# Context products moved between the stages of a four-block decoder, and paired score rows in its ReLU layer

## The chip, the cores and the metric

The program runs on one core of one Trainium2 chip. All data is float32. The metric is the device time of one execution in microseconds (us); kernels are compared by the median of several executions.

The engines are named as the profile names them: PE is TensorE's matrix multiplication and PEld its weight loads, DVE is VectorE, ACT is ScalarE, POOL is GpSimd, SP is the engine that issues the transfers here. SBUF is the on-chip memory, PSUM the matmuls' output memory, HBM the outside memory.

## The reference, cut to what matters

A decoder with four blocks works on `x` of 16 x 64 rows with 512 values. Every block has three parts: attention, attention to a second sequence (the context), and a feed-forward layer. Each part gets the layer-normalised `x` and its result is added to `x`:

```python
x = x + L0_attn(ln(x));  x = x + L0_xattn(ln(x), ctx);  x = x + L0_ffn(ln(x))
x = x + L1_attn(ln(x));  x = x + L1_xattn(ln(x), ctx);  x = x + L1_ffn(ln(x))
x = x + L2_attn(ln(x));  x = x + L2_xattn(ln(x), ctx);  x = x + L2_ffn(ln(x))
x = x + L3_attn(ln(x));  x = x + L3_xattn(ln(x), ctx);  x = x + L3_ffn(ln(x))
```

The parts that the change touches compute this:

- `L1_attn`, `L2_attn`: causal attention, 32 query heads over 8 key heads, 16 values per head. `L2_attn` also turns queries and keys by position (rotary).
- `L1_xattn`: attention to the context with 32 heads of 128 values, with a bias per head and a mask. Its keys `ctx @ Wk` and values `ctx @ Wv` depend on the context alone.
- `L2_xattn`: attention with one head of 512 values; `q = xn @ Wq.T + bq`, `k = ctx @ Wk.T + bk`, and the values are the context itself. `k` depends on the context alone too.
- `L1_ffn`: `h = relu(xn @ w1.T) * keep`, `out = h @ w2t`. `keep` is 1 for one of every 32 hidden values: the one with the largest score in `xn @ c1.T @ c2.T`, a product of rank 16.

## The kernel before

The 1024 rows of `x` stay in SBUF as eight tiles of 128 rows. The kernel is a row of stages, one after another, with a barrier between two of them, and almost every stage walks over the eight tiles. Each engine has its own program in a stage; the order on an engine is the order in which the code is written, and semaphores order the engines against each other. There is no scheduler. The stages, with the names that tiles of theirs carry in the profile: `l0a`, `l0x`, `l0f` (first block), `l1a`, `l1x`, `l1f` (second), `l2a`, `l2x`, `l2f` (third), `l3a`, `l3x`, `l3f` (fourth).

**Context products of `l1x`.** The keys and values of the biased attention are computed ahead, in earlier stages, and stored in HBM. There are 128 units: eight groups of eight key units and eight value units. Helper `Fill` (L2000 on) holds them: `unit` is the TensorE work (a key unit has 4 matmuls of 128 columns by 512, a value unit 8 of 64 columns by 512), `copy` or `copy_act` brings the result from PSUM to SBUF on VectorE or ScalarE, `store` issues the transfer to HBM and behind the last unit of a kind the load of the next group's weights. Two numbers say which stage does which unit: `l0x` does `HELD` to `HELD_X`, 72 to 112, and `l0f` does 113 to 127. In `l0x` five units stand in the opening, four at the end, and 32 in the tiles, one behind each of the four steps of a tile (`WITHIN`, called at the end of a step as `filled(n, c, 1)`):

```python
BEFORE, WITHIN = KC + 1, {(0, 1): 0, (1, 1): 1, (2, 1): 2, (3, 1): 3}
```

A step of `l0x` is: transposition of a softmaxed key block (`turn`, into the one bank `l0x_pt`, copied out by ScalarE before the next one), keys of the next tile, transposition, queries of the next tile, transposition, context product, transposition, values of the next tile.

**The two small attentions** `l1a` and `l2a` are one function, `stage_small_attn` (L3668). On TensorE a tile `n` of the loop is: projections of tile `n+1` (`project`), transposition of the normalised tile `n+2`, output projection of tile `n-1` (`out`), in `l2a` the two rotation products, the probabilities of tile `n` turned in two halves (`turns`, L3787), scores of tile `n+1` first half (`scores`, L3778), attention product of tile `n` (L3799), scores second half. VectorE does the softmax of a tile in 12 passes, in `l2a` also the rotation of the next tile; it can't start before the scores. ScalarE does the exponentials and copies; between the two exponentials of a tile stand the copies of the next tile's queries, keys and values.

**`l2x`** (`stage_l2_xattn`, L3266) loads five weights and inputs at its start and for each tile projects the queries and the keys (16 matmuls of 128 by 128 each), adds the biases on ScalarE, takes the scores, softmax, the transposed probabilities, and the product with the context. The normalisation of tile `n+1` stands ahead of the exponential of tile `n` on ScalarE. Its transposition is followed by the projections on TensorE, and both stand between the scores and the transposition of the probabilities:

```python
pe.wait_ge(q_biased, n + 2); pe.wait_ge(k_biased, n + 2)     # scores of tile n, L3331
...
f.turn(pe, n + 1); project(n + 1, 1 - u)                      # L3314, L3322
pe.wait_ge(p_ready, n + 2)                                    # then transpose p, L3338
```

**`l1f`** (`stage_l1_ffn`, L2550) works on four chunks of 448 hidden values for each tile. For each chunk TensorE does 4 matmuls of 128 by 448 (`l1f_ph`, L2609) and one score matmul with 16 rows (`l1f_pi`, L2614) from the rank-16 product `low`; VectorE finds the largest score of each 32 and masks the hidden values. Both `ph` and `pi` have two banks, used in turn.

## Time and profile before

| | us |
|---|---|
| median of three runs (lowest, highest) | 4292.85 (4287.7, 4294.64) |
| the profiled execution's own time | 4291.77 |
| its span in the trace | 4289.9 |
| PE busy in the span | 3957.4 (92%) |
| DVE busy | 2181.7 (51%) |
| ACT busy | 1427.2 (33%) |
| DMA queue q1, share of 16 engines | 14.2% |
| mean granted TensorE clock of the span | 0.96 of full speed |

The stages that the change touches lie, by the names in the trace, at about 600 to 1065 us (`l0x`), 1065 to 1215 (`l0f`), 1215 to 1380 (`l1a`), 1960 to 2230 (`l1f`), 2230 to 2428 (`l2a`) and 2428 to 2536 (`l2x`).

The profile takes one execution. A float32 matmul of the code appears as two MATMUL instructions in the trace ("x8" for 4 matmuls). Their ends are modelled and neighbouring matmuls overlap, so what a group of matmuls costs is read from its start to the start of the next group behind it, not from its duration. The granted clock is the share of full speed that TensorE was allowed: it has two levels, 1.2 and 2.4 GHz, and a mean between 0.5 and 1 says that a stretch had both.

### The profile page before, as it was taken

The numbers are of one execution on the slowest core, as the hardware profiler recorded it, in microseconds if no ns is written. First come the engines' busy times: TensorE is split into PE (matmuls) and PEld (weight loads), VectorE is DVE, ScalarE is ACT, GpSimd is POOL, SyncE is SP. The second block draws the span as 40 slices with busy tenths as digits, with TensorE's granted clock in tenths as the row PEclk, the third lists the DMA queues.
The fourth block names the chain that finished last, engine by engine and source line by source line (L and its number), as shares of the span: only waits on it lengthen the run. The fifth ranks groups of instructions, "written<-read, shape, count | busy, mean of one in ns | idle before, by whom it ended". The sixth has DMA issues, their size and how long they took to land. (4 is left out here: it accounts for less than half of the span.)

```text
span 4289.9 us, 50949 instructions
## 1 busy us (share of the span) xinstructions
PE 3957.4 (92%) x18954; PEld 2122.3 (49%) x18954; DVE 2181.7 (51%) x3810; ACT 1427.2 (33%) x2586; POOL 313.2 (7%) x288
## 2 busy tenths in 40 slices
PE   8788989998988999999988779699999999999997
PEld 3333335554455555554446564355555445555554
DVE  0887755552247322224548418865655555444433
ACT  3777735552223211111113234311111133322232
POOL 1011002111001000000000111000000000000000
PEclk9999999999988999999998889999999999999998
DMA  4111121112001423211000121111001011111100
GB/s 184 44 40 36 60 68 38 35 35 72 30 28 50 161 101 108 99 35 70 0 27 1 40 100 34 46 41 40 20 20 40 1 66 35 35 35 40 55 15 23
DMA packets 133914, 215.09 MB, mean 50 GB/s; under 512 B 42704, under 2 KB 95056, under 8 KB 123072
## 3 DMA queue, kind: packets, MB, share of 16 engines
q1 hardware_dynamic: 133696, 212.06, 14.2%
q8 instruction: 152, 2.49, 0.2%
q14 instruction: 66, 0.54, 0.0%
HBM read 167.99 MB, written 44.04 MB: 49 GB/s over the span
## 5 line engine op out<-in xcount | busy, mean ns | idle before, releaser
L930 PE MATMUL l3a_po<-l3a_wo,l3a_cT 128*128 128x512 f32 x512 | 230.7, 604 | 3.1 <-ACT l3a_cT L1067 2.9
L436 PE MATMUL l1x_pj<-kvT,l1x_wq 128*128 128x512 f32 x512 | 228.3, 599 | 0.7 <-ACT kvT L240 0.7
L481 PE MATMUL l1x_po<-l1x_wo,l1x_cT 128*128 128x512 f32 x512 | 226.2, 596 | 1.2 <-issue 1.2
L819 PE MATMUL l3x_pj<-kvT,l3x_wq 128*128 128x512 f32 x512 | 225.5, 594 | 0.0
L819 PE MATMUL l3a_pj<-kvT,l3a_wq 128*128 128x512 f32 x512 | 224.9, 592 | 0.0
L577 DVE TENSOR_TENSOR x<-x,l1x_po 128x512 f32<-128x512 f32 x64 | 44.1, 689 | 266.9 <-PE l1x_po L481 266.9
L930 PEld LDWEIGHTS l3a_po<-l3a_wo,l3a_cT 128*128 128x128 f32 x512 | 95.6, 192 | 121.4 <-issue 110.9
L819 PEld LDWEIGHTS l3a_pj<-kvT,l3a_wq 128*128 128x128 f32 x512 | 95.5, 190 | 111.5 <-issue 111.4
L819 PEld LDWEIGHTS l3x_pj<-kvT,l3x_wq 128*128 128x128 f32 x512 | 95.5, 190 | 111.4 <-issue 111.4
L481 PEld LDWEIGHTS l1x_po<-l1x_wo,l1x_cT 128*128 128x128 f32 x512 | 95.7, 192 | 110.9 <-issue 110.9
L436 PEld LDWEIGHTS l1x_pj<-kvT,l1x_wq 128*128 128x128 f32 x512 | 94.6, 190 | 110.2 <-issue 107.2
L194 POOL TENSOR_TENSOR norm_rstd<-norm_half,minus_half 128x1 f32<-128x1 f32 x70 | 42.4, 607 | 1358.9 <-DVE norm_half L189 1358.9
L930 PE MATMUL l3x_po<-l3x_wo,l3x_cT 128*128 128x512 f32 x256 | 117.6, 602 | 0.7 <-issue 0.7
L930 PE MATMUL l3x_pc<-l3x_wo,l3x_cT 128*128 128x512 f32 x256 | 115.1, 592 | 0.0
L1196 DVE TENSOR_TENSOR x<-x,l3a_po 128x512 f32<-128x512 f32 x56 | 38.5, 687 | 149.6 <-PE l3a_po L930 149.6
L1631 ACT ACTIVATE l0a_signs<-l0a_lowest_a,l0a_scalars 128x1376 uint16<-128x1376 uint16 x68 | 98.1, 1442 | 47.9 <-DVE l0a_lowest_a L1755 47.1
L531 ACT COPY l1x_cT<-l1x_pa 128x512 f32<-128x512 f32 x64 | 34.4, 589 | 238.4 <-PE l1x_pa L470 238.4
L1740 DVE TENSOR_SCALAR_CACHE_REDUCE l0a_keep<-l0a_keep,l0a_scalars 128x1376 uint16<-128x1376 uint16 x64 | 105.4, 1646 | 3.2 <-DVE l0a_scalars L1746 1.1
L2609 PE MATMUL l1f_ph<-l1f_w,l1f_xT 128*128 128x448 f32 x256 | 104.1, 550 | 1.3 <-DMA l1f_w<-in_L_ffn_w 1.3
L2637 PE MATMUL l1f_po<-l1f_w,l1f_hT 128*128 128x512 f32 x224 | 102.4, 603 | 0.0
L2045 DVE COPY l0x_fill_kv<-l0x_fill 128x512 f32<-128x512 f32 x41 | 28.4, 692 | 144.6 <-PE l0x_fill L2035 92.0
L1740 DVE TENSOR_SCALAR_CACHE_REDUCE l0a_keep<-l0a_a,l0a_scalars 128x1376 uint16<-128x1376 uint16 x60 | 98.8, 1646 | 4.1 <-DVE l0a_scalars L1746 2.1
(529 smaller groups left out, 7760.0 us busy)
## 6 DMA issues: line engine op xcount, KB each, us to landing
l1x_kb<-l1x_keys SPq DMA_DIRECT2D x32, 512.0 KB, 4.8
l1x_vb<-l1x_values SPq DMA_DIRECT2D x32, 512.0 KB, 3.4
l1x_keys<-l0a_kv SPq DMA_DIRECT2D x40, 256.0 KB, 2.0
fill_wk<-in_L_xattn_Wk SPq DMA_DIRECT2D x8, 1024.0 KB, 5.5
kvT<-in_L_xattn_Wv SPq DMA_DIRECT2D x8, 1024.0 KB, 5.8
l1x_values<-l0a_kv SPq DMA_DIRECT2D x32, 256.0 KB, 2.3
l1x_wq<-in_L_xattn_Wq SPq DMA_DIRECT2D x8, 1024.0 KB, 4.9
l1x_sbias<-in_L_xattn_bias SPq DMA_DIRECT2D x8, 1024.0 KB, 7.4
```

Of the source, the lines that this page charges most:

```text
L194: self.nc.gpsimd.tensor_tensor(self.rstd[:, t:t + 1], self.half[:, t:t + 1], self.m.minus_half[:, 0:1], ALU.pow).then_inc(self.root_ready, 1)
L436: mm = pe.matmul(pj[:, j, :], wq[:, u, k, h * DH:(h + 1) * DH], m.kvT[:, k, 1, 512 * j:512 * (j + 1)], start=k == 0, stop=k == KC - 1)
L481: mm = pe.matmul(po[:, t % 2, :], cT[:, u, h, t * P:(t + 1) * P], wo[:, u, h, :], start=h == 0, stop=h == GH - 1)
L531: nc.scalar.copy(dst, pa[:, z, :].rearrange("p (t s) -> p t s", s=S)).then_inc(a_copied, 1)
L577: nc.vector.tensor_tensor(m.x[:, t, :], m.x[:, t, :], po[:, t % 2, :], ALU.add).then_inc(added, 1)
L819: mm = pe.matmul(pj[:, j, :], wq[:, u, k, h * DH:(h + 1) * DH], m.kvT[:, k, 1, 512 * j:512 * (j + 1)], start=k == 0, stop=k == KC - 1)
L930: mm = pe.matmul(outs[t % 2][:, :], cT[:, h, t * P:(t + 1) * P], wo[:, u, h, :], start=h == 0, stop=h == GH - 1)
L1196: nc.vector.tensor_tensor(m.x[:, t, :], m.x[:, t, :], outs[t % 2][:, :], ALU.add).then_inc(added, 1)
L1631: ins = nc.scalar.activation(signs[:, :], words, ACT.Sign, bias=at[:, :], scale=-1.0, accum_out=total[:, :])
L1740: nc.vector.tensor_scalar(below, words, found[:, :], 0.0, ALU.is_lt, ALU.add, accum_out=cnt[:, :]).then_inc(link, step.next())
L2609: mm = pe.matmul(ph[:, c % 2, 0:CH1], f.xT[:, u, k, :], w1[:, k, c * CH1:(c + 1) * CH1], start=k == 0, stop=k == KC - 1)
L2637: mm = pe.matmul(f.po[:, :], hT[:, j, :], w2[:, j, :], start=j == 0, stop=j == HC1 - 1)
```

## The change

There are four parts.

1. `l0x` gives up eight of its 41 units: `WITHIN` has no entry for the second step of a tile. `HELD_X` goes from 113 to 105, `l0f` does 105 to 119 (seven value units and eight key units, fifteen as before), and `l1a` does the last eight, 120 to 127, all value units, one for each tile. There the unit uses the bank of the output projection (`f.po`), ScalarE copies it, and SP stores it.
2. `l2a` computes the keys of `l2x`, all eight tiles at once, in eight units of 4 matmuls of 128 by 512, one for each tile of `l2a`, also in the bank `f.po`; ScalarE adds the bias. `l2a` also loads all weights of `l2x` and its context. These buffers and the keys `kT` outlive the stage. `l2x` loads nothing and has no key projection. It now normalises and turns two tiles ahead, its query projection is cut in two halves in two banks, one ahead of the transposition of the probabilities and one behind it, and the transposed probabilities have a bank of their own.
3. In both small attentions the second exponential of a tile stands ahead of the copies of the next tile's queries, keys and values on ScalarE.
4. In `l1f` the rank-16 weights are stored twice, for partitions 0 to 15 and 32 to 47, so that `low` has 48 rows (16 of them zero) and the scores of two chunks come from two matmuls that use different rows of the array and different banks. The pair stands ahead of the chunk's hidden values; the second pair waits until VectorE has read the scores of chunk 1.

```diff
-HELD, HELD_X = UNITS - 7 * 2 * GH, UNITS - FILL + 1
+HELD, HELD_X, HELD_F = UNITS - 7 * 2 * GH, UNITS - T - FILL + 1, UNITS - T
-BEFORE, WITHIN = KC + 1, {(0, 1): 0, (1, 1): 1, (2, 1): 2, (3, 1): 3}
+BEFORE, WITHIN = KC + 1, {(0, 1): 0, (2, 1): 1, (3, 1): 2}
...
+                def scores(n, c):                                   # l1f
+                    if c == 0:
+                        pe.wait_ge(low_copied, n + 2)
+                        pe.wait_ge(chunk_done, NCH1 * n + 1)
+                    else:
+                        pe.wait_ge(scores_read, n + 2)
+                    for i in range(2):
+                        rows = slice(32 * i, 32 * i + LOW1)
+                        mm = pe.matmul(pi[:, i, 0:CH1], low[rows, :], wc2[rows, c // 2, :], start=True, stop=True)
+                        mm.then_inc(score_ready, 1)
...
                 def body(n, u):                                     # l2x, TensorE
-                    pe.wait_ge(q_biased, n + 2)
-                    pe.wait_ge(k_biased, n + 2)
+                    pe.wait_ge(q_biased, 2 * n + 3)
                     pe.wait_ge(s_read, n + 1)
                     for c in range(KC):
-                        mm = pe.matmul(pS[:, 0:P], qT[:, c, :], kT[:, c, :], start=c == 0, stop=c == KC - 1)
+                        mm = pe.matmul(pS[:, 0:P], qT[:, c, :], kT[:, c, n * P:(n + 1) * P], start=c == 0, stop=c == KC - 1)
                     mm.then_inc(s_ready, 1)
-                    if not last(n):
-                        pe.wait_ge(pT_ready, n + 1)
-                        f.turn(pe, n + 1)
-                        project(n + 1, 1 - u)
+                    if n + 1 < T:
+                        project(n + 1, 0)
+                    if n + 2 < T:
+                        f.turn(pe, n + 2)
                     pe.wait_ge(p_ready, n + 2)
-                    pe.transpose(f.pt[:, 0:P], p[:, :], m.ident[:, :]).then_inc(p_turned, 1)
+                    pe.wait_ge(pT_ready, n + 1)
+                    pe.transpose(pp[:, 0:P], p[:, :], m.ident[:, :]).then_inc(p_turned, 1)
+                    if n + 1 < T:
+                        project(n + 1, 1)
...
+                def unit(n):                                        # small attention, TensorE
+                    if n == 0:
+                        pe.wait_ge(next_loaded, 32)
+                    pe.wait_ge(f.out_copied, n + 1)
+                    for k in range(KC):
+                        mm = pe.matmul(f.po[:, :], wk2[:, k, (n // 2) * P:(n // 2 + 1) * P],
+                                       m.kvT[:, k, 0, 512 * (n % 2):512 * (n % 2 + 1)], start=k == 0, stop=k == KC - 1)
+                    mm.then_inc(unit_ready, 1)
+
+                def context_unit(n):
+                    pe.wait_ge(f.out_copied, n + 1)
+                    fill.unit(pe, HELD_F + n)
...
                     turns(n, 0)
                     turns(n, 1)
+                    if context:
+                        context_unit(n)
+                    if follower:
+                        unit(n)
                     if within(n + 1):
                         scores(n + 1, 0)
...
                     exps(n, 0)                                      # small attention, ScalarE
                     if within(n + 2):
                         f.norm(act, n + 2)
+                    exps(n, 1)
                     if within(n + 1):
                         copies(n + 1, 1 - u)
-                    exps(n, 1)
```

The order of TensorE's instructions shows three places where this moves work. First a tile of `l1a`, from the turned probabilities (`l1a_pS<-ident`) through the scores (`l1a_kM,l1a_qT`) and the attention product (`l1a_pT,l1a_vB`) to the next projection; before:

```order
L3787 MATMUL l1a_pS<-ident,l1a_sc 128x128 x16
L3778 MATMUL l1a_pS<-l1a_kM,l1a_qT 64x128 x16
L3799 MATMUL l1a_pt<-l1a_pT,l1a_vB 32x4x64 x8
L3778 MATMUL l1a_pS<-l1a_kM,l1a_qT 64x128 x16
L3746 MATMUL l1a_pq<-l1a_xT,l1a_wq 128x128 x16
```

and now, where `l1a_po<-kvT` is the value unit:

```order
L3812 MATMUL l1a_pS<-ident,l1a_sc 128x128 x16
L2034 MATMUL l1a_po<-kvT 64x512 x8
L3803 MATMUL l1a_pS<-l1a_kM,l1a_qT 64x128 x16
L3824 MATMUL l1a_pt<-l1a_pT,l1a_vB 32x4x64 x8
L3803 MATMUL l1a_pS<-l1a_kM,l1a_qT 64x128 x16
L3771 MATMUL l1a_pq<-l1a_xT,l1a_wq 128x128 x16
```

The unit's 8 matmuls have come in between the turned probabilities and the scores of the next tile; nothing else in the row has moved. In `l2a` the same place gets the 4 matmuls of the key unit.

Second a tile of `l2x` on TensorE: scores (`l2x_pS`), transposition of a normalised tile (`l2x_pt<-ident,l2x_xn`), query and key projections (`l2x_pq`, `l2x_pk`), transposed probabilities (`l2x_p`), product with the context (`l2x_po`); before:

```order
L3331 MATMUL l2x_pS<-l2x_kT,l2x_qT 128x128 x4
L265 MATMUL l2x_pt<-ident,l2x_xn 128x128 x4
L3314 MATMUL l2x_pq<-l2x_xT,l2x_wq 128x128 x16
L3322 MATMUL l2x_pk<-kvT,l2x_wk 128x128 x16
L3338 MATMUL l2x_pt<-ident,l2x_p 128x128
L3343 MATMUL l2x_po<-l2x_ctx,l2x_pT 128x512
L3331 MATMUL l2x_pS<-l2x_kT,l2x_qT 128x128 x4
```

and now:

```order
L3329 MATMUL l2x_pS<-l2x_kT,l2x_qT 128x128 x4
L3321 MATMUL l2x_pq<-l2x_xT,l2x_wq 128x128 x8
L265 MATMUL l2x_pt<-ident,l2x_xn 128x128 x4
L3337 MATMUL l2x_pp<-ident,l2x_p 128x128
L3321 MATMUL l2x_pq<-l2x_xT,l2x_wq 128x128 x8
L3342 MATMUL l2x_po<-l2x_ctx,l2x_pT 128x512
L3329 MATMUL l2x_pS<-l2x_kT,l2x_qT 128x128 x4
```

The 16 matmuls of the key projection are gone, half of the 16 query matmuls now stand behind the transposed probabilities, and the transposition of the normalised tile stands behind a projection instead of ahead of it.

Third a tile of `l1f` on TensorE, from the projection to rank 16 (`l1f_pc`) on, with the output products (`l1f_po`), hidden values (`l1f_ph`) and scores (`l1f_pi`); before:

```order
L2601 MATMUL l1f_pc<-l1f_xT,l1f_wc 16x128 x4
L2637 MATMUL l1f_po<-l1f_w,l1f_hT 128x512 x6
L2609 MATMUL l1f_ph<-l1f_w,l1f_xT 128x448 x4
L2614 MATMUL l1f_pi<-l1f_wc,l1f_low 128x448
L2609 MATMUL l1f_ph<-l1f_w,l1f_xT 128x448 x4
L2614 MATMUL l1f_pi<-l1f_wc,l1f_low 128x448
L265 MATMUL l1f_pt<-ident,l1f_xn 128x128 x4
L2609 MATMUL l1f_ph<-l1f_w,l1f_xT 128x448 x4
L2614 MATMUL l1f_pi<-l1f_wc,l1f_low 128x448
L2626 MATMUL l1f_pt<-ident,l1f_h 128x128 x4
```

and now:

```order
L2607 MATMUL l1f_pc<-l1f_xT,l1f_wc 48x128 x4
L2651 MATMUL l1f_po<-l1f_w,l1f_hT 128x512 x6
L2619 MATMUL l1f_pi<-l1f_wc,l1f_low 128x448 x2
L2627 MATMUL l1f_ph<-l1f_w,l1f_xT 128x448 x8
L265 MATMUL l1f_pt<-ident,l1f_xn 128x128 x4
L2619 MATMUL l1f_pi<-l1f_wc,l1f_low 128x448 x2
L2627 MATMUL l1f_ph<-l1f_w,l1f_xT 128x448 x4
L2640 MATMUL l1f_pt<-ident,l1f_h 128x128 x4
```

Four single score matmuls behind the chunks have become two pairs ahead of them.

## Rows read from the trace of the kernel before

**Rows 1.** Busy time by stretch: start:end and length, engines' busy us, clock, DMA share, GB/s.
```profile
600.00:1065.00 465.00, 441.55 (x2212) 222.34 (x2209) 233.42 (x324) 207.22 (x360) 79.55 (x80) 0.98 0.14 43
...
1215.00:1380.00 165.00, 139.80 (x1440) 105.35 (x1440) 116.36 (x131) 63.05 (x97) 19.07 (x17) 0.87 0.05 17
...
1960.00:2230.00 270.00, 259.73 (x755) 119.49 (x756) 128.89 (x222) 35.12 (x65) 15.39 (x18) 0.99 0.08 30
...
2230.00:2428.00 198.00, 161.35 (x1475) 120.14 (x1473) 140.02 (x178) 63.10 (x97) 17.19 (x16) 0.84 0.04 15
...
2428.00:2536.00 108.00, 84.56 (x628) 72.85 (x628) 18.48 (x70) 34.45 (x102) 13.76 (x15) 0.96 0.09 36
```

**Rows 2.** Timeline, stage `l0x`, second step of a tile: start, duration, engine, line, output and inputs.
```profile
814.19 3.65 PE L2035 MATMUL l0x_fill<-kvT 128*64 128x512 f32 x16
...
815.21 1.06 ACT L2357 ACTIVATE l0x_q<-l0x_q 128x1024 f32<-128x1024 f32 x1
...
817.77 0.66 PE L2249 MATMUL l0x_pt<-ident,l0x_ke 128*128 128x128 f32 x4
```

**Rows 3.** Timeline, stage `l1a`, one tile at full clock, TensorE and VectorE.
```profile
1300.97 1.23 DVE L3936 SCALAR_TENSOR_TENSOR l1a_sc<-l1a_pS,causal 128x1024 f32<-128x1024 f32 x1 [1.23 <-PE l1a_pS L3778]
...
1309.92 3.60 PE L3807 MATMUL l1a_po<-l1a_wo,l1a_oT 128*128 128x512 f32 x8
...
1313.50 1.22 DVE L3953 TENSOR_TENSOR l1a_sc<-l1a_sc,l1a_inv 128x1024 f32<-128x1024 f32 x1
...
1314.78 1.09 PE L3787 MATMUL l1a_pS<-ident,l1a_sc 128*128 128x128 f32 x8 [0.39 <-DVE l1a_sc L3953]
...
1316.20 1.10 PE L3778 MATMUL l1a_pS<-l1a_kM,l1a_qT 32*64 32x128 f32 x32 [0.33 <-DVE l1a_kM L3916]
...
1317.37 1.23 DVE L3936 SCALAR_TENSOR_TENSOR l1a_sc<-l1a_pS,causal 128x1024 f32<-128x1024 f32 x1 [1.23 <-PE l1a_pS L3778]
```

**Rows 4.** Timeline, stage `l1a`, two TensorE rows outside the full clock.
```profile
1252.69 5.45 PE L3746 MATMUL l1a_pq<-l1a_xT,l1a_wq 128*128 128x128 f32 x32
...
1370.07 6.41 PE L3807 MATMUL l1a_po<-l1a_wo,l1a_oT 128*128 128x512 f32 x8 [0.69 <-ACT l1a_oT L3884]
```

**Rows 5.** Timeline, TensorE, `l0x` paired 64-row matmuls, then the `l1f` score matmul.
```profile
806.75 1.13 PE L2218 MATMUL l0x_pj<-l0x_cx,l0x_wk 64*128 64x512 f32 x4
...
807.81 0.66 PE L2249 MATMUL l0x_pt<-ident,l0x_ke 128*128 128x128 f32 x4
...
2035.30 1.01 PE L2614 MATMUL l1f_pi<-l1f_wc,l1f_low 16*128 16x448 f32 x2
...
2036.25 3.27 PE L2609 MATMUL l1f_ph<-l1f_w,l1f_xT 128*128 128x448 f32 x8
```

**Rows 6.** Timeline, stage `l2a`, TensorE: first half of the scores of four tiles.
```profile
2265.87 1.50 PE L3778 MATMUL l2a_pS<-l2a_kM,l2a_qT 32*64 32x128 f32 x32 [2.27 <-issue]
...
2311.15 1.10 PE L3778 MATMUL l2a_pS<-l2a_kM,l2a_qT 32*64 32x128 f32 x32 [2.11 <-DVE l2a_qT L3922]
...
2330.55 1.34 PE L3778 MATMUL l2a_pS<-l2a_kM,l2a_qT 32*64 32x128 f32 x32 [2.86 <-DVE l2a_qT L3922]
...
2395.38 1.31 PE L3778 MATMUL l2a_pS<-l2a_kM,l2a_qT 32*64 32x128 f32 x32 [2.66 <-DVE l2a_qT L3922]
```

**Rows 7.** Timeline, stage `l2x`, TensorE and VectorE.
```profile
2430.56 5.30 PE L3314 MATMUL l2x_pq<-l2x_xT,l2x_wq 128*128 128x128 f32 x32 [3.27 <-DMA l2x_bq<-in_L_xattn_bq]
...
2440.71 1.13 PE L3331 MATMUL l2x_pS<-l2x_kT,l2x_qT 128*128 128x128 f32 x8 [1.28 <-issue]
...
2441.68 0.60 PE L265 MATMUL l2x_pt<-ident,l2x_xn 128*128 128x128 f32 x4
...
2442.95 3.84 PE L3314 MATMUL l2x_pq<-l2x_xT,l2x_wq 128*128 128x128 f32 x32 [0.67 <-ACT l2x_xT L270]
...
2528.18 1.13 PE L3331 MATMUL l2x_pS<-l2x_kT,l2x_qT 128*128 128x128 f32 x8 [1.00 <-issue]
...
2531.13 0.29 DVE L3404 TENSOR_SCALAR l2x_p<-l2x_p,l2x_tot 128x128 f32<-128x128 f32 x1
```

More of the change, by code:

```diff
@@ L1876, in _ @@
                 sp.dma_start(wb[:], w_b).then_inc(loaded, 16)
-                for g in range(HELD_X, UNITS):
+                for g in range(HELD_X, HELD_F):
                     fill.store(sp, g)
@@ L2006, in __init__ @@
         self.kv = st.sb("fill_kv", [P, STAGED, 512])
-        self.banks = [st.ps(f"fill{i}", [P, 512]) for i in range(banks)]
+        self.banks = banks if isinstance(banks, list) else [st.ps(f"fill{i}", [P, 512]) for i in range(banks)]
         self.wk_loaded, self.wv_loaded = st.dma_sem("fill_wk_loaded"), st.dma_sem("fill_wv_loaded")
@@ L2611, in chunk @@
                     mm.then_inc(hid_ready, 1)
-                    if c == 0:
-                        pe.wait_ge(low_copied, n + 2)
-                    pe.matmul(pi[:, c % 2, 0:CH1], low[:, :], wc2[:, c * CH1:(c + 1) * CH1],
-                              start=True, stop=True).then_inc(score_ready, 1)
                 def hidden_turn(n, g):
@@ L2645, in _ @@
                     u = n % 2
+                    scores(n, 0)
                     chunk(n, u, 0)
@@ L2650, in _ @@
                         f.turn(pe, n + 1)
+                    scores(n, 2)
                     chunk(n, u, 2)
@@ L2667, in low_copy @@
                     act.wait_ge(low_ready, n + 2)
-                    nc.scalar.copy(low[:, :], pc[0:LOW1, 0:P]).then_inc(low_copied, 1)
+                    nc.scalar.copy(low[:, :], pc[0:LOW_ROWS, 0:P]).then_inc(low_copied, 1)
                 f.act(act, 0, 0)
@@ L2705, in body @@
                               ALU.is_equal).then_inc(link, chain.next())
+                        if c == 1:
+                            dve.wait_ge(link, chain.behind)
+                            dve.sem_inc(scores_read, 1)
                         dve.wait_ge(link, chain.behind)
@@ L3315, in project @@
                                            start=k == 0, stop=k == KC - 1)
                     mm.then_inc(q_ready, 1)
-                    pe.wait_ge(k_biased, n + 1)
-                    if n == 0:
-                        pe.wait_ge(k_loaded, 32)
-                    for c in range(KC):
-                        for k in range(KC):
-                            mm = pe.matmul(pk[:, c * P:(c + 1) * P], wk[:, k, c * P:(c + 1) * P],
-                                           m.kvT[:, k, 0, n * P:(n + 1) * P], start=k == 0, stop=k == KC - 1)
@@ L3384, in body @@
                 def body(n, u):
-                    if n >= 2:
-                        dve.wait_ge(f.added, n)
-                        ahead.moments(dve, n - 2)
                     chain.at(3 * n)
@@ L3404, in body @@
                     nc.vector.tensor_scalar(p[:, :], p[:, :], tot[:, 1:2], None, ALU.mult).then_inc(p_ready, 1)
+                    if n >= 2:
+                        dve.wait_ge(f.added, n)
+                        ahead.moments(dve, n - 2)
                 every_tile(body)
@@ L3731, in _ @@
                 sp.dma_start(wo[:], w_o).then_inc(loaded, 16)
+                if context:
+                    for g in range(HELD_F, UNITS):
+                        fill.store(sp, g)
+                    fill.finish(sp)
+                if follower:
+                    sp.dma_start(wk2[:], follower["wk"]).then_inc(next_loaded, 16)
+                    sp.dma_start(bk2[:], follower["bk"]).then_inc(next_loaded, 16)
+                    for key in ("wq", "bq", "ctx"):
+                        sp.dma_start(m.next[key][:], follower[key]).then_inc(given_loaded, 16)
+                    sp.wait_ge(given_loaded, 48)
             @block.gpsimd
@@ L4088, in _layout @@
     a["causal"] = np.tile(tri, (2, 1))
-    a["L1_ffn_c1_w"] = rows(f["L1_ffn_c1_w"].T)
-    a["L1_ffn_c2_w"] = f["L1_ffn_c2_w"].T
+    c1 = np.zeros((D, LOW_ROWS), np.float32)
+    c2 = np.zeros((LOW_ROWS, NCH1 // 2, CH1), np.float32)
+    for i in range(2):
+        c1[:, 32 * i:32 * i + LOW1] = f["L1_ffn_c1_w"].T
+        c2[32 * i:32 * i + LOW1] = f["L1_ffn_c2_w"].T.reshape(LOW1, NCH1 // 2, 2, CH1)[:, :, i]
+    a["L1_ffn_c1_w"], a["L1_ffn_c2_w"] = rows(c1), c2
     a["L1_ffn_w1"] = rows(f["L1_ffn_w1"].T)
```

151 lines of the change are left out of this document (85 added, 66 removed).

## The prediction

> **What bounds the kernel now.** I read the table of busy time by stretch first. It says where TensorE is the bound: 441.6 of 465 us in `l0x`, 259.7 of 270 in `l1f`, at nearly full clock [rows 1]. In the two small attentions it is busy 85% and 81% at a mean clock of 0.87 and 0.84, and in `l2x` 78% [rows 1]. So removed matmuls count in `l0x` and `l1f` unless a wait takes their place, and in the other three the chain between the engines must be read from the timeline.
>
> In `l1a` a tile at full clock takes 16.40 us (1300.97 to 1317.37, the start of VectorE's softmax in two tiles) and TensorE idles in it only twice, 0.39 and 0.33 us, so it works 15.68. VectorE idles 1.23 us. It is one loop: scores, softmax, turned probabilities, scores [rows 3]. In `l2a` TensorE waits 2.3 to 2.9 us for VectorE's rotation ahead of each tile's scores, and the mean tile takes (2395.38 - 2265.87) / 6 = 21.6 us, though one at full clock takes 19.40 [rows 6]. In `l2x` a tile takes (2528.18 - 2440.71) / 7 = 12.50 us, eight such starts [rows 7].
>
> **The change, part by part**, against the profiled execution: 4289.9 us of span, 4291.8 its own time, 1.1 below the median of 4292.9.
>
> *`l0x`, eight units fewer.* A unit costs 3.58 us there (814.19 to 817.77) [rows 2]. It covers ScalarE: that is busy with the query exponential until 815.21 + 1.06 = 816.27, then copies the first transposition (0.6), and the second one needs that copy. Without the unit TensorE would do the first transposition and the keys in 0.6 + 1.06 us (the keys by 806.75 to 807.81 [rows 5]) and want the bank at 815.84; it gets it at 816.92. So 1.1 us of wait come in for 3.58 removed: 2.5 gained, in seven tiles. The last tile has neither keys nor exponentials; one copy of about 0.9 is uncovered there, 2.7 gained. Sum **-20**. Bounds: -29 if no wait comes, -11 if a second wait of the same size follows. `l0f` trades one value unit for one key unit at the same work: nothing, and its one more weight load has the DMA queues nearly to itself.
>
> *`l1a`, eight units more.* The unit stands on the loop. New loop at full clock: 13.75 us from the softmax's start to its last multiplication's end (1300.97 to 1313.50 + 1.22), 1.15 for the second half's turns, 3.58 for the unit, 1.17 from scores to softmax: 19.65 against 16.40 [rows 3]. TensorE's own work, 15.68 + 3.58 = 19.26, is just below. The mask product and the score wait that now end the loop are hidden. So +3.25 for each of five tiles: +16. [...] Two tiles: 2 x 3.25 - 1.6 = +5. In the last tile TensorE has idled for VectorE and the output product runs at 1.2 GHz, 6.41 us [rows 4] against 3.60 [rows 3]. The unit takes about 5.3 there, covers a ScalarE copy (about 1), and gives 2.8 back: +1.5. Sum **+22.5**, bounds +13 (clock up throughout) and +36 (eight times 3.6, two of them doubled). Behind the unit on TensorE are the scores, the attention product and the next projections, and VectorE waits for the scores. ScalarE's 0.6 us copy of the unit is done while TensorE does the scores.
>
> *`l1f`, pairs.* A score matmul costs 0.95 us (2035.30 to 2036.25), four for each tile. The nearest row for a pair on different array rows is that of `l0x`: two matmuls of 64 rows by 512 columns in 1.06 us [rows 5]. For 448 columns that is 0.93 to 1.06; I take 1.0. Saved 0.9 in each of 16 pairs: **-14.4**, bounds 0 (the pair runs one after the other) and -15.5. No loss is to be had, since the same matmuls are issued. VectorE, busy 129 of 270 us [rows 1], gets its scores earlier; it should have read those of chunk 1 some 6 us into the tile, and TensorE comes to that wait after 8. By the Trainium skill ("TensorE: Matmul & The Clock Gate", Part 3, "The mechanism") matmuls on different row groups start about 4 ns apart, so that a pair costs like one matmul; that would be 0.95 here and -15.2, an estimate. The row of `l0x` says a bit more, 1.06.
>
> *`l2a`, eight key units.* Each is as much as the output product, 3.60 us [rows 3], but 2.86 us of it fall into the wait ahead of the scores. A full-clock tile has 19.40 - 2.86 = 16.54 us of TensorE work [rows 6], so the new tile is 16.54 + 3.60 = 20.14, bound by TensorE, with VectorE ready 0.7 earlier. That is shorter than the mean of 21.6 now: the low-clock stretches begin right behind the waits of 2.7 to 2.9 us (scores of 1.50, 1.34 and 1.31 us in place of 1.10 [rows 6]), and these waits are filled. Six tiles: 120.8 against 129.5, -8.7. The first tile: 3.60 - 2.27 = +1.3. The last, reckoned as in `l1a`: +2. Sum **-5.4**, bounds -8 and, if the clock keeps falling as now, +16. The Trainium skill ("TensorE: Matmul & The Clock Gate", "HAM oscillation — how this bites in real kernels") has idle gaps of TensorE throttle the clock, and keeping it busy as the cure. By that rule the sum is the one above, without it +16. The loads of `l2x` join a queue in a stage with a DMA share of 0.04 [rows 1] and are wanted at the earliest 30 us later: nothing.
>
> *The two exponentials ahead of the copies.* In full-clock tiles VectorE doesn't wait for the second exponential: nothing. In low-clock tiles it does; that is within the terms above. The copies come about 1 us later, and the rotation products that need them some 2.5 us after that.
>
> *`l2x`.* TensorE's work for a tile becomes: scores 0.97 (2440.71 to 2441.68), query projection 3.7 (3.84 with overlap), transposition 0.5, probabilities 0.27, context product 0.95: 6.4 us. The softmax takes 2531.13 + 0.29 - 2528.18 = 3.24 us from the scores' start [rows 7]; TensorE now has 0.97 + 1.85 + 0.5 = 3.3 us of work ahead of the turned probabilities, so that they are just in time, and the second half projection covers the copy of them. The bias of that half is added during the context product. ScalarE has about 4 us of work in a tile. I take 6.5 for 12.50: 7 x -6.0 = -42. At the start the wait of 3.27 us for the weights [rows 7] and the key projection go, and a second transposition comes: the first scores stand 10.8 us behind the stage's start instead of 15.2, -4.4. Sum **-46**; bounds -50 and -34 (8 us a tile, if ScalarE's row of waits decides).
>
> Together -20 + 22.5 - 14.4 - 5.4 - 46.4 = **-64 us**: 4228 for the profiled execution, 4229 for the median.
>
> **Rivals.**
>
> A. The clock does not come up: the units in the small attentions cost their full price or more. `l1a` +33, `l2a` +16, the rest as above: -32, so 4261. For it: both stages lose their clock now. Against it: the five middle tiles of `l1a`, whose waits are 0.3 and 0.4 us, all run at full clock.
>
> B. The pairs of `l1f` run one after the other, the rest as forecast: -49, so 4244. Against it: the pair in `l0x`. For it: nothing here shows 16-row matmuls side by side. The Trainium skill ("TensorEngine Tiling (Array Packing)", "Gotcha 1: PSUM Pressure") forbids row tiles of one bank to work at once; these write two banks, so the rule does not bring this case about.
>
> C. `l2x` becomes bound by ScalarE's order: its copy of the turned tile and the first half of the biases stand ahead of the copy of the probabilities. With 3 us more a tile, 9.5, the stage gains 25: -43, so 4250. Against it: these copies fit into TensorE's second half projection.
>
> D. Slower: the units cost more than the other parts save. The others save 20 + 14.4 + 46.4 = 81 us, over 16 units 5.0 us each. From there on the kernel is slower. With all units and the TensorE work around them at 1.2 GHz a unit is 7.2 us and a tile some us more: about +115, so 4327. Against it: the same middle tiles; more work can hardly lower a clock that idling lowers.
>
> **How the numbers follow.** Forecast 0.72, A 0.10, B 0.05, C 0.09, D 0.04. The likeliest gives 4229. Its own range by the bounds, not all at one end: 4212 to 4248. A, B and C lie at 4261, 4244 and 4250, so the range is 4210 to 4262. About 0.2% (8.6 us) is what a measurement can tell from no change. All cases but D are far beyond it: faster 0.95, same 0.02, slower 0.03. Of D one hundredth is put to no change, and one more comes from A.
>
> **What the changed profile would show.** `l0x`: TensorE waits about 1.1 us for ScalarE's copy in the step without a unit, and the stage is 20 us shorter. `l1a`: softmax starts 19.6 us apart in the middle tiles. `l1f`: a pair of score matmuls in 1.0 us, a tile 1.9 shorter. `l2a`: tiles of 20.1 us, no wait ahead of the scores, mean clock above 0.9. `l2x`: score starts 6.5 us apart. The prediction is wrong if `l2a` tiles are above 22 us, if `l2x` tiles are above 8, or if the stage `l1a` grows by more than 36.

## The result and the profile after

The changed kernel takes 4216.28 us (median of 4, 4214.54 to 4218.02) against 4292.53 (median of 4, 4287.7 to 4294.64) for the kernel before on the same chip: a ratio of 0.9822, 95% interval 0.981 to 0.9834. The forecast was 4229, 13 us too high and inside its range. The profiled execution took 4217.35 us, its span 4215.4.

Stage lengths, from the first instruction of a stage to the first of the next one, in the two traces:

| stage | before | after | difference | forecast |
|---|---|---|---|---|
| `l0x` | 465.3 | 443.9 | -21.4 | -20 |
| `l0f` | 155.5 | 154.35 | -1.2 | 0 |
| `l1a` | 163.8 | 182.8 | +19.0 | +22.5 |
| `l1x` | 580.05 | 580.3 | +0.2 | 0 |
| `l1f` | 267.5 | 251.45 | -16.1 | -14.4 |
| `l2a` | 198.1 | 189.15 | -9.0 | -5.4 |
| `l2x` | 112.3 | 63.8 | -48.5 | -46.4 |
| rest of the span | | | +2.5 | 0 |
| sum | | | -74.5 | -64 |

The busy time of the same stretches (start:end and length, busy us of PE, PEld, DVE, ACT and POOL, granted clock, DMA share, GB/s), which answers to [rows 1]:

```profile
595.00:1039.00 444.00, 413.74 (x2096) 213.25 (x2096) 228.36 (x315) 207.15 (x361) 81.00 (x85) 0.98 0.12 39
...
1193.50:1376.30 182.80, 161.88 (x1568) 109.24 (x1568) 116.12 (x130) 66.16 (x104) 18.94 (x17) 0.93 0.08 27
1956.60:2208.00 251.40, 242.88 (x752) 118.71 (x752) 125.39 (x218) 33.51 (x64) 14.29 (x16) 0.98 0.08 31
2208.00:2397.00 189.00, 169.31 (x1536) 118.99 (x1536) 139.04 (x178) 66.58 (x104) 18.53 (x17) 0.93 0.10 38
2397.00:2461.00 64.00, 53.53 (x376) 45.70 (x376) 20.70 (x74) 29.28 (x72) 14.53 (x16) 0.90 0.00 1
```

The clock is the first thing to see: 0.93 in both small attentions, from 0.87 and 0.84. In `l2a` TensorE is busy 8 us longer in a stage 9 us shorter. Of the 2.5 us in the rest of the span 1.9 stand in `l2f`, which no part of the change touches: 248.8 us before, 250.7 in this trace, 249.0 in the second trace of the changed kernel.

The timeline of `l0x` in the changed kernel, at the second step, which has lost its unit:

```profile
807.15 1.13 PE L2222 MATMUL l0x_pj<-l0x_cx,l0x_wk 64*128 64x512 f32 x4
...
808.55 0.58 ACT L2370 COPY l0x_kT<-l0x_pt 128x512 f32<-128x512 f32 x1
809.18 0.66 PE L2253 MATMUL l0x_pt<-ident,l0x_ke 128*128 128x128 f32 x4 [0.90 <-ACT l0x_kT L2370]
```

The bracket is the wait that came in for the unit of [rows 2]: 0.90 us, for a copy that had to stand behind the exponential.

The first unit of `l1a`, one tile in the middle, and the last tile of the stage, in the changed kernel; they answer to [rows 3, 4]:

```profile
1224.11 4.42 PE L2034 MATMUL l1a_po<-kvT 128*64 128x512 f32 x16
1228.46 1.10 PE L3803 MATMUL l1a_pS<-l1a_kM,l1a_qT 32*64 32x128 f32 x32
...
1231.53 3.84 PE L3771 MATMUL l1a_pq<-l1a_xT,l1a_wq 128*128 128x128 f32 x32
...
1302.58 3.65 PE L2034 MATMUL l1a_po<-kvT 128*64 128x512 f32 x16
1306.17 1.10 PE L3803 MATMUL l1a_pS<-l1a_kM,l1a_qT 32*64 32x128 f32 x32
...
1307.34 1.23 DVE L3992 SCALAR_TENSOR_TENSOR l1a_sc<-l1a_pS,causal 128x1024 f32<-128x1024 f32 x1 [4.41 <-PE l1a_pS L3803]
...
1326.91 1.22 DVE L3992 SCALAR_TENSOR_TENSOR l1a_sc<-l1a_pS,causal 128x1024 f32<-128x1024 f32 x1 [4.41 <-PE l1a_pS L3803]
...
1362.48 5.21 PE L2034 MATMUL l1a_po<-kvT 128*64 128x512 f32 x16
...
1367.62 1.07 PE L3824 MATMUL l1a_pt<-l1a_pT,l1a_vB 128*32 128x256 f32 x16
...
1369.40 3.70 PE L3851 MATMUL l1a_po<-l1a_wo,l1a_oT 128*128 128x512 f32 x8 [0.70 <-ACT l1a_oT L3940]
```

The softmaxes start 19.57 us apart (16.40 before), and VectorE now waits 4.41 us for the scores where it waited 1.23: the unit is on the loop. In the last tile the unit takes 5.14 us until the attention product starts, and that product and the output product behind it are at full clock, 3.70 instead of 6.41.

`l2a` in the changed kernel, a unit and the scores of two tiles, against [rows 6]:

```profile
2264.07 3.60 PE L3834 MATMUL l2a_po<-kvT,l2a_next_wk 128*128 128x512 f32 x8
2267.60 1.10 PE L3803 MATMUL l2a_pS<-l2a_kM,l2a_qT 32*64 32x128 f32 x32
...
2287.51 1.10 PE L3803 MATMUL l2a_pS<-l2a_kM,l2a_qT 32*64 32x128 f32 x32
```

Behind the first scores of the stage no wait stands ahead of any others, and all last 1.10; the tiles are 19.91 us apart (the last one 19.52). `l1f` and `l2x` in the changed kernel, against [rows 5, 7]:

```profile
2026.01 1.02 PE L2619 MATMUL l1f_pi<-l1f_wc,l1f_low 16*128 16x448 f32 x4
2026.96 6.28 PE L2627 MATMUL l1f_ph<-l1f_w,l1f_xT 128*128 128x448 f32 x16
...
2408.53 1.16 PE L3329 MATMUL l2x_pS<-l2x_kT,l2x_qT 128*128 128x128 f32 x8 [0.72 <-ACT l2x_qT L3357]
2409.53 1.95 PE L3321 MATMUL l2x_pq<-l2x_xT,l2x_wq 128*128 128x128 f32 x16
2411.32 0.60 PE L265 MATMUL l2x_pt<-ident,l2x_xn 128*128 128x128 f32 x4
2411.86 0.33 PE L3337 MATMUL l2x_pp<-ident,l2x_p 128*128 128x128 f32 x1
2412.03 1.96 PE L3321 MATMUL l2x_pq<-l2x_xT,l2x_wq 128*128 128x128 f32 x16
2413.82 1.02 PE L3342 MATMUL l2x_po<-l2x_ctx,l2x_pT 128*128 128x512 f32 x2
2414.70 1.16 PE L3329 MATMUL l2x_pS<-l2x_kT,l2x_qT 128*128 128x128 f32 x8
```

A pair (x4 are two matmuls of the code) takes 0.95 us, exactly what one single matmul took. A middle tile of `l2x` is 6.17 us without one wait in it; only the last two tiles wait for the softmax, 0.38 and 2.17 us.

### The profile page after: what moved, and what is told of

It is laid out like the page before. It is cut to its first block and busy times, and to the rows that moved or that the text cites. A ratio compares the mean times of both kernels' runs of the same rounds, so it can differ in the third digit from the quotient of the medians.

```text
span 4215.4 us, 50580 instructions
## 1 busy us (share of the span) xinstructions
PE 3910.7 (93%) x18762; PEld 2088.9 (50%) x18762; DVE 2173.2 (52%) x3802; ACT 1425.1 (34%) x2570; POOL 313.7 (7%) x288
## 5 line engine op out<-in xcount | busy, mean ns | idle before, releaser
L1503 PE MATMUL l0a_pg<-kvT,fill_wk 128*128 128x512 f32 x160 | 74.5, 618 | 25.1 <-ACT l0a_s L1580 13.5
```

Source lines behind the costliest of these rows:

```text
L1503: mm = pe.matmul(banks[b], wk[:, k, h * DH:(h + 1) * DH], m.kvT[:, k, 0, 512 * j:512 * (j + 1)], start=k == 0, stop=k == KC - 1)
```

## The experiments

Each is the changed kernel with one thing altered, but for the last, which goes on from the one ahead of it. The whole of a kernel can't show 3 us: in the traces the stages ahead of `l0x`, which are the same everywhere, end between 595.2 and 598.3. So stage lengths are compared. Where the code of a stage is the same they agree within 0.5 us, with exceptions that no edit explains (`l0x` 445.5 instead of 443.9 in two traces, `l0f` up to 155.2 instead of 154.4 in the same two, `l1a` 185.9 instead of 182.9 and `l1f` 249.8 instead of 251.4 in one, `l2a` 190.0 and 190.5 instead of 188.7 to 189.4 in two, `l2x` 63.8 instead of 62.7 in two). So a difference of 2 to 3 us in one stage of one trace needs rows of its own.

**Context units back in `l0x`.**

```diff
-HELD, HELD_X, HELD_F = UNITS - 7 * 2 * GH, UNITS - T - FILL + 1, UNITS - T
+HELD, HELD_X, HELD_F = UNITS - 7 * 2 * GH, UNITS - FILL + 1, UNITS
-WITHIN = {(0, 1): 0, (2, 1): 1, (3, 1): 2}
+WITHIN = {(0, 1): 0, (1, 1): 1, (2, 1): 2, (3, 1): 3}
```

> The changed kernel with its eight context units back in l0x (four for each tile there, none in l1a); key units of l2a, pairs of l1f and the new l2x stay. Theory (a unit costs 3.6 us less the wait that it covers): l0x and l0f give back the 21.4 and 1.2 us that they won, and l1a gives up the 19.0 that it lost, so the whole is 3.6 us slower than the changed kernel, 4220, with l0x at 465 us, l1a at 164 to 165 us and its middle tiles at 16.4. Rival (the units keep TensorE's clock up in l1a, so that the stage gains nothing without them): l1a stays above 170 us and the whole is 4226 or more.

4217.24 us (4215.09 to 4219.16), ratio to before 0.9823 (0.981 to 0.9837). `l0x` 465.0, `l0f` 156.1, `l1a` 164.0 with a clock of 0.87. The stages went back as the theory said: +22.8 and -18.9 against the changed kernel. So moving eight units is worth about 4 us, 2.85 us saved for each in the first block and 2.4 paid in `l1a`; in the medians of the whole it can't be told from nothing. The rival falls.

**Order of the exponentials undone.** `copies(n + 1)` ahead of `exps(n, 1)` again.

> The changed kernel with one thing undone: in both small attentions ScalarE copies the next tile's projections ahead of the second exponential again. Theory: VectorE does not wait for that exponential in a full-clock tile, so l1a and l2a stay within 1 us of 182.8 and 189.1 and the whole within 2 us of 4216. Rival (the order made the room for the units, and with the copies first VectorE gets the second exponential late): l1a and l2a 0.6 us longer for each tile, up to 5 us each, the whole 4221 to 4226.

4216.8 us (4214.76 to 4221.38), `l1a` 182.9, `l2a` 189.0. The order is worth nothing here.

**`l2x` in its old order**, with its keys still made in `l2a`:

```diff
                     if n + 1 < T:
-                        project(n + 1, 0)
-                    if n + 2 < T:
-                        f.turn(pe, n + 2)
+                        pe.wait_ge(pT_ready, n + 1)
+                        f.turn(pe, n + 1)
+                        project(n + 1)
                     pe.wait_ge(p_ready, n + 2)
-                    pe.wait_ge(pT_ready, n + 1)
-                    pe.transpose(pp[:, 0:P], p[:, :], m.ident[:, :]).then_inc(p_turned, 1)
-                    if n + 1 < T:
-                        project(n + 1, 1)
+                    pe.transpose(f.pt[:, 0:P], p[:, :], m.ident[:, :]).then_inc(p_turned, 1)
...
```

(`project` makes all four column blocks of the queries again, and ScalarE's program is in its old order too.)

> The changed kernel with the stage l2x in the order that it had before (one tile turned ahead, the whole query projection behind the next turn, one bank for it), but with its keys still made in l2a and its weights loaded there. It parts the 48.5 us that l2x won. Theory: a tile before was TensorE's work of 9.8 us and 2.7 us of waits, so without the key projection (3.8 us) and its four bias additions the tile is 8 to 9 us against 12.50 before and 6.17 now; the stage is 80 to 88 us, the whole 4233 to 4241: the keys are worth 25 to 33 us, the order 16 to 24. Rival (the old tile was bound by the chain of scores, softmax, turn and biases and not by TensorE's work): the tile stays above 10 us, the stage above 95, the whole 4248 or more.

4228.23 us (4227.02 to 4231.89), ratio 0.9849 (0.9834 to 0.9864). The stage takes 75.7 us. TensorE's timeline in that kernel, one tile:

```profile
2418.38 1.16 PE L3327 MATMUL l2x_pS<-l2x_kT,l2x_qT 128*128 128x128 f32 x8
2419.94 0.63 PE L265 MATMUL l2x_pt<-ident,l2x_xn 128*128 128x128 f32 x4 [0.40 <-ACT l2x_xn L259]
2421.24 3.84 PE L3319 MATMUL l2x_pq<-l2x_xT,l2x_wq 128*128 128x128 f32 x32 [0.68 <-ACT l2x_xT L270]
2424.92 0.27 PE L3334 MATMUL l2x_pt<-ident,l2x_p 128*128 128x128 f32 x1
2425.54 1.13 PE L3337 MATMUL l2x_po<-l2x_ctx,l2x_pT 128*128 128x512 f32 x2 [0.35 <-ACT l2x_pT L3360]
2426.59 1.16 PE L3327 MATMUL l2x_pS<-l2x_kT,l2x_qT 128*128 128x128 f32 x8
```

The tile is 8.21 us, inside the theory's 8 to 9; its three waits of 0.40, 0.68 and 0.35 us are what the new order hides. From start to start the steps that hold them are 0.56, 0.76 and 0.45 us longer than in the new order, 1.77 of the 2.04; the rest is in the product (0.17) and the projection (0.10). But the stage fell short of the 80 to 88 us: the theory forgot its start. The first scores stand 9.5 us behind the stage's start (15.2 before, 11.2 now), because the weights are there. Of 48.5 us the keys, their biases and the loads bring 36.6, and the order 12 to 13 (2.04 in each of seven tiles, less 1.7 for the second transposition at the start).

**Pairs undone.** The stage `l1f` of before.

> The changed kernel with the stage l1f as it was before: four score matmuls of 16 rows in a tile, each behind its chunk's hidden product, and no pairs. Theory: everything that l1f won comes from the pairs, two matmuls in the time of one: l1f goes back to 267.5 us from 251.5, the whole to 4232. Rival (part of it came from VectorE's earlier start or from the state that the stages before left): l1f below 264 us, the whole below 4229.

4236.12 us (4235.1 to 4237.4), ratio 0.9869 (0.9853 to 0.9886). `l1f` 267.9, everything else as in the changed kernel. The whole 16 us come from the stage's own code.

**The pair on the same rows.**

```diff
-                        rows = slice(32 * i, 32 * i + LOW1)
+                        rows = slice(0, LOW1)
```

> The changed kernel with both matmuls of a pair on the same 16 rows of the array (rows 0 to 15), in the same place of the order and with the same sizes; the second half of the scores is thereby made from the wrong columns of the weights. It tells whether the row groups or the new order give the 16 us. Theory: the two matmuls then run one after the other, a pair takes 1.7 to 1.9 us instead of 0.95, l1f is 266 to 268 us and the whole 4228 to 4232. Rival (the gain came from issuing the two back to back, which saves the switch of the array between 128 rows and 16): the pair takes 0.95 to 1.2 us, l1f below 256, the whole below 4221.

4227.9 us (4226.73 to 4233.53), ratio 0.9853 (0.9837 to 0.987). TensorE's timeline in that kernel:

```profile
2029.42 1.76 PE L2620 MATMUL l1f_pi<-l1f_wc,l1f_low 16*128 16x448 f32 x4
2031.12 6.28 PE L2628 MATMUL l1f_ph<-l1f_w,l1f_xT 128*128 128x448 f32 x16
```

The pair takes 1.70 us, `l1f` 263.35. The theory's pair was right and its stage 3 us too long: two matmuls one after the other take 1.70 and not 1.90, so that 0.20 us of each single one is spent once for a row of 16-row matmuls, and not for each of them. The row groups bring 0.75 in each of 16 pairs, 12.0 us (measured 263.35 - 251.45 = 11.9), the change of order the other 4.6, of which 16 x 0.20 = 3.2 stand in the score matmuls. The rest stands beside them: in the trace before, the four hidden products of a tile, from start to start, take 3.10, 3.20, 3.10 and 3.10 us, the one with a score matmul on both sides being the longest; in the changed kernel the one with none beside it takes 3.01 (2008.10 to 2011.11). Half of the score groups are gone, so fewer products have one beside them. What it is that costs 0.20 inside and 0.1 beside such a group, no run tells.

**Every unit twice.** `for k in list(range(KC)) * 2` in the units of both small attentions.

> The changed kernel with the matmuls of each of the 16 units in l1a and l2a done twice (8 for each key unit, 16 for each context unit; same values). Theory: both stages are bound by TensorE at full clock now, so each unit costs its full 3.45 to 3.6 us again: l1a 182.8 + 28 = 211, l2a 189.1 + 28 = 217, tiles 23.1 and 23.4 us, granted clock of both stages above 0.93, the whole 4272. Rival (more work in these stages brings the clock up further, or fills waits that are left): less than 2.5 us for each unit, the whole below 4257. Second rival (the units cost more than their length, because ScalarE's copies or the clock suffer): over 4.5 us each, 4288 or more.

4268.08 us (4267.6 to 4270.33), ratio 0.9945 (0.9929 to 0.9962). The two stages in that kernel (columns as above):

```profile
1193.60:1403.80 210.20, 189.48 (x1696) 118.50 (x1696) 116.15 (x130) 66.21 (x104) 18.95 (x17) 0.94 0.07 24
2235.50:2451.50 216.00, 195.95 (x1600) 130.10 (x1600) 139.15 (x178) 66.52 (x104) 18.60 (x17) 0.94 0.09 34
```

27.4 and 26.9 us more, 3.4 for each unit, at a clock of 0.94. A second unit costs nearly its full length (3.53 to 3.6 us), so nothing much is left in a tile to hide it. Both rivals fall.

**A quarter of each key unit.** `for k in range(1)` in `unit`, three of the four matmuls left out.

> The changed kernel with one of the four matmuls in each key unit of l2a (0.9 us instead of 3.6; the keys of l2x are thereby incomplete). It tells whether the units hold TensorE's clock up there. Theory (what is left of a unit does not fill the wait ahead of the scores, and the clock falls as it did before): TensorE waits about 2 us ahead of each tile's scores, the mean clock of the stage is below 0.88, some tiles take over 20.5 us, and l2a stays within 4 us of the 189.1 us that it takes with full units, though 21 us of work are gone. Rival (the clock does not depend on the unit, the order of the exponentials or chance keeps it up): clock above 0.93 and tiles of 19.4 us or less, l2a at 185 us or below. If the unit were simply work on the path, l2a would be 168.

4215.72 us (4211.31 to 4217.26), ratio 0.9818 (0.9802 to 0.9834): as fast as the changed kernel. `l2a` in that kernel, the stretch and two tiles:

```profile
2211.50:2398.00 186.50, 157.33 (x1488) 116.06 (x1488) 138.11 (x178) 66.26 (x104) 17.44 (x17) 0.88 0.10 39
```

```profile
2286.79 1.70 PE L3803 MATMUL l2a_pS<-l2a_kM,l2a_qT 32*64 32x128 f32 x32 [2.00 <-issue]
2288.42 1.94 PE L3824 MATMUL l2a_pt<-l2a_pT,l2a_vB 128*32 128x256 f32 x16
2290.29 1.98 PE L3803 MATMUL l2a_pS<-l2a_kM,l2a_qT 32*64 32x128 f32 x32
...
2328.73 1.10 PE L3803 MATMUL l2a_pS<-l2a_kM,l2a_qT 32*64 32x128 f32 x32 [2.00 <-issue]
```

In three of the seven tiles 2.0 us of wait stand ahead of the scores again (0.3 to 1.4 in the others). Behind two of the three the clock falls, and these tiles take 22.5 and 22.1 us; the others take 18.1 to 19.4. Three quarters of the units' work are gone, 21 us, and the stage is 2.6 us shorter; its six tiles behind the first are even 1.9 us longer (121.0 against 119.1). So in `l2a` a unit costs almost nothing because it fills a wait *and* because that wait costs clock. The order of the exponentials, unchanged here, doesn't hold the clock up by itself. But this kernel's `l2a` is also 11.6 us shorter than the stage before, with a quarter of the filler. No run has the new order and no units at all, so how much of that the order brings where the waits are left stays open.

**Four units moved to where TensorE waits.**

```diff
+                    if n in edge and not (follower and n == 0):         # edge is (0, T - 1)
+                        either(n)                                       # context_unit or unit
                     turns(n, 0)
                     turns(n, 1)
-                    if context:
-                        context_unit(n)
-                    if follower:
-                        unit(n)
+                    if n not in edge:
+                        either(n)
...
                 rotate(0)
+                if follower:
+                    unit(0)
                 scores(0, 0)
...
```

(`follower` is `l2a`. The last unit of each stage goes to the bank `pq`.)

> The changed kernel with four of its sixteen units put where TensorE waits: in l1a the first and the last one ahead of the tile's turns, in l2a the first ahead of the first scores and the last ahead of the last tile's turns (the last ones in the free bank of the query projection). TensorE idles 5.8 us ahead of the last tile's turns in both stages, 2.5 us ahead of the first turns in l1a and 2.6 us ahead of the first scores in l2a. Theory: the two last units disappear into the idle time: 5.2 and 4.8 us less, and the output product behind them may fall back to 1.2 GHz, which costs up to 2.8 us in each; the first ones save 2.5 us each. Together 7 to 15 us less, the whole 4201 to 4209, l1a 174 to 178 us, l2a 182 to 186. Rival (the edges are bound by VectorE's and ScalarE's chain, and the low clock behind it takes back what the unit gave): l1a and l2a shorter by less than 2 us each, the whole 4212 or more.

4218.83 us (4216.05 to 4219.44), ratio 0.9826 (0.9812 to 0.9839): no gain. The stages tell two stories: `l1a` 176.9, 5.9 less, and `l2a` 192.6, 3.5 more. TensorE in `l2a` of that kernel, second tile and end:

```profile
2241.81 1.98 PE L3805 MATMUL l2a_pS<-l2a_kM,l2a_qT 32*64 32x128 f32 x32 [2.26 <-issue]
2243.72 1.94 PE L3826 MATMUL l2a_pt<-l2a_pT,l2a_vB 128*32 128x256 f32 x16
...
2247.50 5.88 PE L3773 MATMUL l2a_pq<-l2a_xT,l2a_wq 128*128 128x128 f32 x32
...
2378.16 1.97 PE L3814 MATMUL l2a_pS<-ident,l2a_sc 128*128 128x128 f32 x8 [2.39 <-DVE l2a_sc L4033]
...
2386.63 6.24 PE L3865 MATMUL l2a_po<-l2a_wo,l2a_oT 128*128 128x512 f32 x8 [0.69 <-ACT l2a_oT L3962]
```

The unit taken out of the first tile hid in the wait ahead of the first scores, but left a wait of 2.26 us in its old place, and the clock fell behind it: the tile behind that wait takes 24.6 us instead of 19.9, with its own unit in both. At the end, the unit hid in the idle time as meant, and the output product fell back to 6.24 us: from the last scores to the end of the stage 30.59 us against 30.57. The theory's 7 to 15 us fell: for the low clock at the end it counted the output product alone (2.5 us), while the attention product (0.9) and the wait for ScalarE's copy that the unit had covered (1.2) come on top, and together that is 4.6 of the unit's 4.8. In `l1a` 5.2 of the 5.9 us come from the first tile. The last unit won nothing there either: from the last scores to the end of the stage it is 30.27 us here and 30.28 in the kernel below that moves the first unit alone.

**The changed kernel again**, beside the next two on one chip.

> The changed kernel itself, beside the next two on the same chip, so that differences of a few us can be read: 4216 us, and stage lengths within 0.5 us of those of its first profile, but for the small attentions, where the clock may come up a few us earlier or later (up to 3 us).

4215.55 us (4214.26 to 4216.36), ratio 0.9817 (0.9803 to 0.983). `l1a` 182.9, `l2a` 188.8, `l2x` 62.7.

**Only the first unit of `l1a` moved** ahead of the first tile's turns.

> The changed kernel with one unit moved: in l1a the first context unit stands ahead of the first tile's turns, where TensorE idles 2.5 us. l2a stays as it is, since a unit taken out of its first tile opened a wait there and the clock fell behind it. Theory: the second tile's first scores come 15.0 us behind the first ones instead of 20.2, as in the kernel with four moved units, and nothing is given back: l1a 177.6 us instead of 182.8, l2a 189, the whole 5 us below the changed kernel. Rival (a hole that is filled here is paid for at the next one, as in l2a): l1a above 180.5, the whole within 2 us of the changed kernel.

4210.06 us (4206.44 to 4212.28), ratio 0.9806 (0.9792 to 0.9819). `l1a` 176.8, `l2a` 188.8. TensorE in `l1a` of that kernel:

```profile
1216.71 3.65 PE L2034 MATMUL l1a_po<-kvT 128*64 128x512 f32 x16
...
1220.30 1.09 PE L3812 MATMUL l1a_pS<-ident,l1a_sc 128*128 128x128 f32 x8
...
1223.01 1.10 PE L3803 MATMUL l1a_pS<-l1a_kM,l1a_qT 32*64 32x128 f32 x32
```

The unit stands in the former hole, the turns behind it take 1.09 instead of 1.97, and the second scores come 15.0 us behind the first instead of 20.2. This kernel beats both: 5.5 us below the changed kernel, and their ranges on the same chip don't touch. 5.2 us of it are the hole. The last tile of `l1a`, where the code is the same, also took 0.9 us less (30.28 against 31.16), at a granted clock of 0.89 against 0.83; no edit explains that.

**Idle time filled with work that nobody reads.** The kernel with the first unit moved, and six more matmuls of 128x512 ahead of the last tile's turns, in both stages:

```diff
+                    if n == T - 1:
+                        pe.wait_ge(q_free, n + 2)
+                        for i in range(6):
+                            pe.matmul(pq[:, :], m.kvT[:, 0, 0, 0:P], wo[:, i % REP, :], start=True, stop=True)
```

> The kernel with the first unit moved, and in the last tile of both small attentions six matmuls of 128x512 more (5.4 us, written to a free bank and read by nobody) in the 5.8 us for which TensorE idles ahead of the turns. They only keep TensorE busy. Theory (idling lowers the clock there): the turns behind take 1.09 us each instead of 1.97 and the last unit 3.6 instead of 5.2 and 4.8; from the last tile's scores to the end of the stage it is 2 to 2.5 us less in each, 4 to 5 us in the whole. Rival (the clock falls in the waits of 0.7 and 1.6 us between the turns anyway, as it did in the kernel with four moved units): the unit or the products behind it run at 1.2 GHz, the ends of the stages are within 1 us of those of the changed kernel, or longer.

4209.77 us (4208.95 to 4212.99), ratio 0.9805 (0.9791 to 0.9818). TensorE at the end of `l2a` in that kernel:

```profile
2369.13 5.31 PE L3867 MATMUL l2a_pq<-l2a_wo,kvT 128*128 128x512 f32 x12
...
2377.80 1.09 PE L3812 MATMUL l2a_pS<-ident,l2a_sc 128*128 128x128 f32 x8 [1.58 <-DVE l2a_sc L4017]
2378.73 3.60 PE L3834 MATMUL l2a_po<-kvT,l2a_next_wk 128*128 128x512 f32 x8
...
2384.04 3.70 PE L3851 MATMUL l2a_po<-l2a_wo,l2a_oT 128*128 128x512 f32 x8 [0.70 <-ACT l2a_oT L3948]
```

In `l2a` everything stays at full clock and the end of the stage is 2.3 us shorter (28.50 from the last scores against 30.83 in the kernel with the first unit moved), as the theory says. In `l1a` it is 30.36 against 30.28: the clock fell in the second turns (1.83 us) and the unit took 4.5. The theory held in one stage of the two, and the whole shows no gain where 4 to 5 us were expected.

## Why the prediction was right

The number isn't owed to errors that cancel. Six stages came out 1.2 to 3.6 us better than forecast each, 13.5 us together, and the rest of the span took 2.7 of it back. The steps were right in kind, and their sizes cautious.

**`l0x`.** The mechanism is shown: a unit of 3.58 us goes, a wait of 0.90 comes. The forecast's wait was 1.1, so 2.7 instead of 2.5 a tile; with `l0f` 2.85 us a unit. The 1.2 us of `l0f` were forecast as nothing, and no experiment says more of them than that they come back with the units, and that the stage's granted clock is 0.94 before and in that run, 0.95 in the changed kernel.

**`l1a`.** Five middle tiles: forecast 19.65 and +16, measured 19.57 and +15.9 (97.9 us from the third scores to the eighth, 82.0 before). The first two tiles cost +3.3 where +5 was forecast. The forecast took 1.6 us off the full-clock price of two tiles, a term that no row of a unit stood behind. The changed kernel shows 4.35 us for the unit at 1224.11, inside which the clock came up. Behind it the projection took 3.84 us instead of 5.45 [rows 4], which is 1.6; but the scores and the attention product ahead of the projection came up too, 3.07 us instead of 5.69 (1228.46 to 1231.53, before 1247.00 to 1252.69). The start of the stage, ahead of the first scores, is 0.5 us shorter. The last tile cost +0.3 where +1.5 was forecast. The unit took 5.14 us there (about 5.3 forecast), and the step that was mis-sized is "gives 2.8 back": it named the output product alone, and the attention product too went from 1.93 to 1.07 us. With it the sum is 5.14 - 1.19 (a wait covered) - 2.71 - 0.86 = +0.4.

**`l1f`.** Forecast 1.0 us for a pair, taken between the bounds 0.93 and 1.06; it is 0.95. The term is 1.7 too small. The pair accounts for 0.8 of it (16 x 0.05); a middle tile is 2.15 us shorter where the pairs alone give 1.9, and the rest is in the hidden products beside them, 12.24 us a tile instead of 12.50. That a pair costs what a single one costs is what the Trainium skill says ("TensorE: Matmul & The Clock Gate", Part 3, "The mechanism"); the trace agrees, 0.95 and 0.95. Rival B had its own run: had the pairs run one after the other, 12 of the 16 us would have been lost.

**`l2a`.** The forecast had 16.54 + 3.60 = 20.14 us a tile and no low clock; it is 19.91 and none. The term came out 3.6 too small: 119.1 us for six tiles against 129.5, -10.4 instead of -8.7, and the last tile +0.4 instead of +2, for the same reason as in `l1a`. That the clock decides here was an argument from rows at two levels, and the quarter units bear it out. One reading was wrong: the forecast has TensorE wait 2.3 to 2.9 us ahead of each tile's scores and puts the low clock behind the waits of 2.7 to 2.9, but its own row of 1.50 us stands behind a wait of 2.27 [rows 6], three of the seven waits are 2.11, and the clock fell behind one of these three too, as the second half of these scores in the kernel before shows:

```profile
2289.32 1.10 PE L3778 MATMUL l2a_pS<-l2a_kM,l2a_qT 32*64 32x128 f32 x32 [2.11 <-DVE l2a_qT L3922]
...
2292.22 1.99 PE L3778 MATMUL l2a_pS<-l2a_kM,l2a_qT 32*64 32x128 f32 x32
```

The remedy, to fill every wait, didn't depend on that. What the units cost and what the clock gives back can be parted by the full-clock tile of 19.40 us [rows 6]: six of them are 116.4 us, so the low clock had cost 13.1 us, and of that the units took 2.7.

**`l2x`.** 6.17 us a tile instead of 6.5, and the first scores 11.2 us behind the start instead of 10.8. The tiles bring 44.3 us instead of 42, the start 4.0 instead of 4.4. Rival C had ScalarE's copies ahead of the probabilities; there is no wait for them but 0.35 us in the last tile.

**The exponentials** were forecast at nothing, and undoing them gave nothing.

**Rivals A and D** priced a unit at 5 us and more. The doubled units give 3.4 at full clock, and the quarter units show why rival A turned round: more work kept the clock up.

## What to carry to other kernels

Price added TensorE work by the wait that it fills and by what the clock does behind that wait: in `l2a` eight units of 3.6 us went into a stage that became 9 us shorter, and with three quarters of their work taken out again it was only 2.6 us shorter still. A filler taken from one place to fill a hole in another opens a hole in its old place; check what stands behind both, which is why the first unit of `l1a` won 5 us when it was moved and two moved in `l2a` lost 3.5. Where work for one tensor doesn't depend on the stage, doing it earlier also takes its loads and biases out of the stage: in `l2x` that was 37 of 48 us, with the units in `l2a` as the price.
